# Expert stage of a fused two-layer decoder: float32 products turned into three float32r passes, and two lookup units moved

## The reference, cut to what matters

```
x = LN(x + self_attention(x))                 # layer 0, 8 heads of 8
x = LN(x + softmax(ctx x^T / sqrt(128)) .. ctx)  # layer 0, "second attention"
x = LN(x + expert(x))                         # layer 0, the stage that is changed
x = LN(x + nf4_attention_and_mlp(x))          # layer 1, weights from 4-bit codes
x = LN(x + cross_attention(x, ctx))           # layer 1
x = LN(x + ternary_mlp(x))                    # layer 1

expert(x): x W^T + b + (x A[:r]^T) B[:, :r]^T, r in (8,16,32,64) chosen per row
           by the largest of four gate scores x gate_w^T + gate_b
```

## Time and profile before

| | us |
|---|---|
| median of 3 runs | 637.84 (637.5 to 638.32) |
| profiled execution, its own time | 637.31 |
| its span | 635.5 |
| TensorE busy in the span | 623.7 |
| VectorE busy | 449.0 |
| ScalarE busy | 388.9 |
| TensorE's granted clock | 1.0 of full |

### The profile page before, as it was taken

The page is one execution under the profiler, slowest core; times in us unless marked ns, Lnnn a source line. Parts: engine busy times, 40 slices in busy tenths (PEclk is TensorE's granted clock), DMA queues, the critical chain, the costliest instruction groups (busy, mean ns, idle before and its releaser), DMA issues.

```text
span 635.5 us, 8677 instructions
## 1 busy us (share of the span) xinstructions
PE 623.7 (98%) x3186; PEld 461.7 (73%) x3186; DVE 449.0 (71%) x714; ACT 388.9 (61%) x564; POOL 64.4 (10%) x116
## 2 busy tenths in 40 slices
PE   9999999999999999999999999999999999999995
PEld 7655555544568887888888888887777888887874
DVE  4788787557778979898987537325675777777467
ACT  2977798656676697786866135223458545667532
POOL 1032132211230000000000000001221000000012
PEclk9999999999999999999999999999999999999999
DMA  7762485303133225343630003029001133200002
GB/s 251 288 214 86 168 277 199 102 0 93 48 104 108 69 77 164 122 138 99 184 108 5 1 0 135 1 92 404 1 1 33 50 101 100 67 0 2 1 34 100
DMA packets 25592, 63.94 MB, mean 101 GB/s; under 512 B 5541, under 2 KB 10725, under 8 KB 24782
## 3 DMA queue, kind: packets, MB, share of 16 engines
q1 hardware_dynamic: 23294, 61.68, 29.8%
q10 hardware_dynamic: 2256, 1.70, 0.9%
HBM read 58.77 MB, written 4.60 MB: 100 GB/s over the span
## 4 chain that ended last, share of the span: by engine, by line
PE 81%; ACT 7%; DVE 4%; DMA 4%; issue 2%; SPq 1%; POOL 0%; POOLq 0%; DVEq 0%; ACTq 0%
PE bank L1121 19%; PE bank L1257 10%; PE bank L1109 5%; PE bank L1108 5%; PE bank L1110 5%; PE bank L960 4%; PE bank L880 4%; PE bank L684 3%; ACT line L1393 3%; DMA b_gu<-in_b_gu 2%; PE bank L990 2%; PE bank L819 2%; PE bank L1199 2%; PE bank L1200 2%; PE bank L1175 1%
## 5 line engine op out<-in xcount | busy, mean ns | idle before, releaser
L1393 ACT ACTIVATE line<-line 128x1024 f32<-128x1024 f32 x87 | 91.3, 1049 | 0.1
L1108 PE MATMUL bank<-xh,wh 128*128 128x512 f32 x224 | 87.5, 391 | 0.0
L1109 PE MATMUL bank<-xl,wh 128*128 128x512 f32 x224 | 87.4, 390 | 0.0
L1110 PE MATMUL bank<-xh,wl 128*128 128x512 f32 x224 | 87.3, 390 | 0.0
L1121 PE MATMUL bank<-wh,xh 128*128 128x512 f32 x176 | 69.8, 396 | 0.2 <-DVE xl L2381 0.2
L1121 PE MATMUL bank<-wh,xl 128*128 128x512 f32 x176 | 68.6, 390 | 0.0
L2381 DVE TENSOR_TENSOR xl<-arena,xh 128x1024 fp32r<-128x1024 f32 (+1 forms) x24 | 28.3, 1178 | 35.7 <-ACT xh L1698 35.5
L1698 ACT ACTIVATE xh<-arena 128x1024 fp32r<-128x1024 f32 (+1 forms) x24 | 24.4, 1022 | 39.6 <-PE bank L1121 35.3
L1110 PEld LDWEIGHTS bank<-xh,wl 128*128 128x128 f32 x224 | 42.1, 188 | 8.9
L1108 PEld LDWEIGHTS bank<-xh,wh 128*128 128x128 f32 x224 | 42.1, 188 | 8.8 <-DVE arena L2283 0.3
L1109 PEld LDWEIGHTS bank<-xl,wh 128*128 128x128 f32 x224 | 42.1, 188 | 8.4
(11 more groups left out here) (287 smaller groups left out, 1354.3 us busy)
## 6 DMA issues: line engine op xcount, KB each, us to landing
codes<-in_c_gu SPq DMA_DIRECT2D x14, 512.0 KB, 5.2
scales<-in_s_gu SPq DMA_DIRECT2D x28, 256.0 KB, 4.0
codes<-in_t_gu SPq DMA_DIRECT2D x8, 512.0 KB, 3.8
codes<-in_c_dn SPq DMA_DIRECT2D x7, 512.0 KB, 4.9
scales<-in_s_dn SPq DMA_DIRECT2D x14, 256.0 KB, 3.9
fold<-in_t_dn SPq DMA_DIRECT2D x1, 3584.0 KB, 15.7
codes<-in_c_qkv SPq DMA_DIRECT2D x6, 512.0 KB, 4.5
scales<-in_t_gu SPq DMA_DIRECT2D x6, 512.0 KB, 4.2
```

The costliest lines, as they stand in the source:

```text
L1108: pe.matmul(dst, wh[:, s, c:c + P], xh[:, k, cols], start=(k == 0), stop=False)
L1109: pe.matmul(dst, wh[:, s, c:c + P], xl[:, k, cols], start=False, stop=False)
L1110: last = pe.matmul(dst, wl[:, s, c:c + P], xh[:, k, cols], start=False, stop=(k == KD - 1))
L1393: nc.scalar.activation(below(slot), below(slot), ACT.Prelu, bias=bias, scale=scale, alpha=alpha).then_inc(bent, 1)
```

## The change

The transposed blocks of the stage's input are written as float32r (`x2_hi`), and VectorE writes what the rounding lost (`x2_low`, into `x2_lo`). VectorE also splits the two weight matrices into high and low parts (`w0_split`, `ag_split`) during the fourth and fifth steps of the second attention. `ranks` and `ffn_W` then make three float32r passes for each of the four k (`x2_products`) in place of one float32 product. The plan of the second attention loses the units of steps 6 and 7, and the expert stage gets one more in its steps 0 and 6. `down_stack_hi` moves behind the last transposes of `attention_out`, `down_stack_low` into gate/up tile 2, and the three late down chunks each move one tile later. Buffers move too: the low parts of the attention matrix (`m_lo`) now stand where `kq_w` was, and the adapter's `ad_high` where the expert stage's input was.

```diff
-LATE = {2: 4, 5: 5, 8: 6}
+LATE = {3: 4, 6: 5, 9: 6}
...
-PLAN = ([0] + [1] * (NT - 1), [2], [0] + [1] * 7, [1] * NT)
+PLAN = ([0] + [1] * (NT - 1), [2], [0] + [1] * 5, [2, 1, 1, 1, 1, 1, 2, 1])
...
                 keys_out(t)
-                if t % 2 == 0:
+                if t in (2, 4):
                     load_scales(C_O + t // 2)
                     load_codes(C_O + 1 + t // 2)
-            load_scales(C_O + NT // 2)
...
-            for c in range(C_O + 1 + NT // 2, C_GU):
+            for c in range(C_O + NT // 2, C_GU):
+                load_scales(c - 1)
                 load_codes(c)
-                load_scales(c)
+            load_scales(C_GU - 1)
...
-                if layer == 2 and b:
-                    pe.wait_ge(xl_ready, b)
+                if NT * (layer - 1) + b > 0:
+                    pe.wait_ge(xl_ready, NT * (layer - 1) + b)
                 transpose_tile(b, x[:, b, :], bank[6])
...
+            def x2_products(dst, b, w_hi, w_lo, last):
+
+                cols = slice(b * P, (b + 1) * P)
+                part = slice(b % KD * P, (b % KD + 1) * P)
+                for k in range(KD):
+                    pe.matmul(dst, x2_hi[:, k, cols], w_hi[k], start=(k == 0), stop=False)
+                    pe.matmul(dst, x2_lo[b // KD][:, k, part], w_hi[k], start=False, stop=False)
+                    ins = pe.matmul(dst, x2_hi[:, k, cols], w_lo[:, k, :], start=False, stop=last and k == KD - 1)
+                return ins
...
-                for k in range(KD):
-                    last = pe.matmul(turn_bank(b)[:, 0:RMAX + NL], xT[:, k, b * P:(b + 1) * P], agT[:, k, :],
-                                     start=(k == 0), stop=(k == KD - 1))
-                last.then_inc(ag_ps, 1)
+                pe.wait_ge(xl_ready, max(KD, b + 1))
+                x2_products(turn_bank(b)[:, 0:RMAX + NL], b, [ag_hi[:, k, :] for k in range(KD)], ag_lo, True).then_inc(ag_ps, 1)
...
-                for k in range(KD):
-                    pe.matmul(bank[FF_BANK[b % 3]][:, :], xT[:, k, b * P:(b + 1) * P], w0T[:, k, :], start=(k == 0), stop=False)
+                x2_products(bank[FF_BANK[b % 3]][:, :], b, w0_hi, w0_lo, False)
...
-                elif t < 4:
-                    down_stack_hi(t - 2)
...
             x1_T_out(NT - 1)
+            down_stack_hi(0)
+            down_stack_hi(1)
             late_first_bends(at_gu(2))
...
+            def x2_low(b):
+
+                dve.wait_ge(xt_ready, NT + b + 1)
+                nc.vector.tensor_tensor(x2_lo[b // KD][:, :, b % KD * P:(b % KD + 1) * P], bank[6][:, :].rearrange("p (k t) -> p k t", k=KD),
+                                        f32(x2_hi[:, :, b * P:(b + 1) * P]), ALU.subtract).then_inc(xl_ready, 1)
+
+            def w0_split(rows):
+
+                for k in rows:
+                    last = nc.vector.tensor_copy(w0_hi[k], w0T[:, k, :])
+                link(last)
+                for k in rows:
+                    nc.vector.tensor_tensor(w0_lo[:, k, :], w0T[:, k, :], f32(w0_hi[k]), ALU.subtract)
+
+            def ag_split():
+
+                dve.wait_ge(in_ffn0, 48)
+                link(nc.vector.tensor_copy(ag_hi, agT))
+                nc.vector.tensor_tensor(ag_lo, agT, f32(ag_hi), ALU.subtract)
+
             for t in range(2, NT + 1):
                 if t < NT:
                     sims_max(t)
+                if t >= 3:
+                    x2_low(t - 3)
                 for u, h in half_plan(2, t, 0):
                     unit_part(u, h)
...
+                if t == 4:
+                    ag_split()
+                    w0_split(range(0, 2))
+                elif t == 5:
+                    w0_split(range(2, KD))
...
-                if t == 4:
-                    down_stack_low()
...
                 hidden(s, j - 2)
+                if j == 2:
+                    down_stack_low()
```

More of the change, by code:

```diff
@@ L217, in decoder_kernel @@
         m_hi = sb("m_hi", [P, KD, D], F32R)
+        with nc.sbuf_tensor("fold_r", [P, NF, D], F32R) as fold_r:
+            pass
         fold = sb("fold", [P, NF, D])
@@ L261, in decoder_kernel @@
         woT, at = carve(arena, at, KD * D)
+        shared_at = at
         shared, at = carve(arena, at, KD * D)
@@ L266, in decoder_kernel @@
         wo0, at = carve(arena, at, D)
+        ag_at = at
         agT, at = carve(arena, at, KD * (RMAX + NL))
@@ L271, in decoder_kernel @@
         bT_d, at = carve(arena, at, D)
+        wk2_at = at
         wk2, at = carve(arena, at, D)
@@ L287, in decoder_kernel @@
         lora_l = wo0
-        ad_high = wh[:, :, :].rearrange("p s c -> p (s c)")[:, 0:FF]
-        m_lo = [arena_r[:, m_at:m_at + D] for m_at in (wk3_at, free_at, free_at + D, wo0_at)]
+        ad_high = arena_r[:, xT_at:xT_at + FF]
+        x2_hi = arena_r[:, xT_at:xT_at + KD * T].rearrange("p (k t) -> p k t", k=KD)
+        x2_lo = [m_hi[:, :, :], wh[:, :, :].rearrange("p s c -> p (s c)").rearrange("p (k t) -> p k t", k=KD)]
+        w0_hi = [arena_r[:, w_at:w_at + D] for w_at in (wk3_at, wk2_at, free_at, free_at + D)]
+        w0_lo = arena_r[:, shared_at:shared_at + KD * D].rearrange("p (k c) -> p k c", k=KD)
+        ag_lo = arena_r[:, ag_at:ag_at + KD * (RMAX + NL)].rearrange("p (k c) -> p k c", k=KD)
         KQ_F, BETA_F, CTX_F = KD, KD + 1, NF
@@ L338, in decoder_kernel @@
         KQ_F0, CTX_SLOT = NF - 6, NF - 2
+        m_lo = [fold_r[:, KQ_F0 + c, :] for c in range(KD)]
+        ag_hi = fold_r[:, CTX_SLOT, 0:KD * (RMAX + NL)].rearrange("p (k c) -> p k c", k=KD)
         assert at <= KQ_F0 * D
@@ L496, in gu_scales_landed, with stacked @@
             eng.wait_ge(in_gus[c % RING], 32 * ((c - C_GU) // RING + 1))
+        def stacked(j, down):
+            return 2 + j + 1 + int(j >= down)
         def gu_slot(j):
@@ L636, in _ @@
                     if n >= 2:
-                        sp.wait_ge(stack_low, 3 + n - 1)
+                        sp.wait_ge(stack_low, stacked(n - 2, 3))
                     sp.dma_start(b_gu[:, n % 2, :], i["b_gu"][n]).then_inc(in_bgu[n % 2], 16)
@@ L1000, in attention_out @@
                     pe.wait_ge(x1_ready, t - 1)
-                pe.wait_ge(xl_ready, t + 1)
+                pe.wait_ge(xl_ready, NT + t + 1)
                 cols = slice(t * P, (t + 1) * P)
@@ L1050, in gu_lora @@
             def gu_lora(j):
-                pe.wait_ge(stack_low, 3 + j + 1)
+                pe.wait_ge(stack_low, stacked(j, 3))
                 if j == 0:
@@ L1070, in x1_T @@
                 elif b == 3:
-                    pe.wait_ge(xl_ready, NT)
+                    pe.wait_ge(xl_ready, 2 * NT)
                 elif b >= 4:
-                    pe.wait_ge(xl_ready, NT + b - 3)
+                    pe.wait_ge(xl_ready, 2 * NT + b - 3)
                 transpose_tile(b, rbuf[:, b % 2, :], bank[X1_BANK[b % 4]])
@@ L1098, in gu_tile @@
                     if p == 0:
-                        pe.wait_ge(xl_ready, NT + NT // 2)
+                        pe.wait_ge(xl_ready, 2 * NT + NT // 2)
                     elif p == 1:
-                        pe.wait_ge(xl_ready, 2 * NT)
+                        pe.wait_ge(xl_ready, 3 * NT)
                     else:
@@ L1211, in t_gate @@
                 if j == 0:
-                    pe.wait_ge(xl_ready, 2 * NT + (tg + 1) * NT // 2)
+                    pe.wait_ge(xl_ready, 3 * NT + (tg + 1) * NT // 2)
                 t_gu_part_of(j, tg, 0, t_ps)
@@ L1558, in _ @@
                 if t >= 2:
-                    x_T_out(NT + t - 2)
+                    x_T_out(NT + t - 2, dst=x2_hi)
                 for u, h in half_plan(2, t, 1):
@@ L2211, in add_lora @@
                 dve.wait_ge(af_ps, n + 1)
-                if n == 0:
-                    dve.wait_ge(scaled, C_DN)
+                if n in (0, KD):
+                    dve.wait_ge(scaled, C_DN - 1 + n // KD)
                 dst = (wsum, woT)[n % 2][:, n // 2, :]
@@ L2225, in down_stack_low @@
             def down_stack_low():
-                dve.wait_ge(stack_hi, 4)
+                dve.wait_ge(stack_hi, 6)
                 nc.vector.tensor_tensor(ad_st[2 * RG:STACK, :], a_down[2 * RG:STACK, :], f32(ad_high[2 * RG:STACK, :]), ALU.subtract).then_inc(stack_low, 1)
             def b_lower(j):
-                dve.wait_ge(stack_hi, 4 + j + 1)
+                dve.wait_ge(stack_hi, stacked(j, 2) + int(j >= 2))
                 part = b_st[RG:2 * RG, j % 2, :]
@@ L2250, in _ @@
             turn_norm(2 * NT - 1)
+            x2_low(NT - 2)
             choose(1)
+            x2_low(NT - 1)
             dve.wait_ge(kq_ps, NT)
```

## The result

The changed kernel is slower: 641.55 us (640.8 to 642.4) against 638.08 (637.5 to 638.64) of before on the same chip, ratio 1.005, 95% interval 1.0035 to 1.0066, some 3.5 us between the medians. Forecast were 638.9 and a range of 636.2 to 642.0. The profiled execution of after took 640.84 with a span of 639.0, 3.5 more than that of before; its granted clock is 0.999.

What follows compares the result with a forecast made beforehand. TensorE, busy 623.7 of 635.5 us, was taken as the bound. Terms -5.1 + 4.0 + 1.6 + 0.3 + 0.3 = +1.1 us gave 638.4 on the profiled execution's 637.31 and 638.9 on the median 637.84; range 636.2 to 642.0.

Steps and rivals of the forecast that it cites:

- rival D: Expert stage's first blocks: VectorE becomes the bound, steps 0 to 2 each late by a unit part; 642.2 us, chance 0.13.
- matrix and rank products: TensorE, eight blocks: twelve float32r passes replace four float32 products; matrix -5.1 us, rank +4.0 us.
- sixth context product: Second attention: the inserted splits make VectorE's probabilities late, so TensorE waits; +1.6 us, bounds nothing to 3.6.
- VectorE in steps 0 to 2: Expert stage: the moved-in chunk and shifted order delay VectorE's work against TensorE's blocks; +0.3 us, 0 to 1.
- step 6 of the expert stage: Expert stage, where the plan adds a unit: no cost forecast, 0.
- gate/up: Start of gate/up: down_stack_hi ahead of tile 2's bends delays the first hidden product; +0.3 us, 0 to 0.8.
- rival B: Rank products: short float32r passes cost 0.22 us, no cheaper than float32; +14.1 instead of +4.0, 649 us, chance 0.14.
- decides the sign from 0.12 a pass on: Rank products: pass time said to settle faster or slower from 0.12 us, each 0.01 making 0.96 us.
- From step 3 on ... VectorE waits for TensorE again.: Expert stage: each block holds 3.4 us more attention_product and down_stack_low (2.02) is gone, so VectorE has room.
- `down_stack_low` ... follows behind the hidden product in a tile that no longer has the late chunk's 3.7: Gate/up: the 2.02 us subtraction goes where the 3.7 us late chunk left; no cost of its own forecast.
- The later LATE positions only swap neighbours: Gate/up: moving the later late down chunks was taken as mere reordering, with no cost or gain forecast.
- wait at a second place for more than a microsecond: TensorE, anywhere besides the sixth context product: such a wait was named as a sign that the forecast is wrong.

Runs made afterwards that it cites:

- e9: Changed kernel with down stack back in the expert stage, step 6's second unit in step 3, splits in second-attention steps 5 and 6: ratio 0.9943 to before.
- e4: Changed kernel with the weight splits in steps 5 and 6 of the second attention instead of 4 and 5: ratio 1.0029 to before.
- e3: Changed kernel with the second unit of the expert stage's step 6 moved to step 3: ratio 1.0032 to before.
- e2: Changed kernel with the down stack's copies and subtraction back in the expert stage, steps 2 to 4: ratio 1.0006 to before.
- e6: Kernel before with only the changed LATE positions, {3: 4, 6: 5, 9: 6}: ratio 0.9981 to before.
- e1: Changed kernel with LATE back as before, {2: 4, 5: 5, 8: 6}: ratio 1.0134 to before.

## Why the prediction was right or wrong

The direction and the number came out inside what was stated, 641.55 in 636.2 to 642.0, but in good part by luck. The upper end of the range was the sum of rival D, which didn't happen; two losses that the sum had at 0 and at +0.3 took its place, and products that came cheaper than forecast offset some of them.

The forecast's +1.1 against the +3.48 of the marks, term by term:

| term | forecast | measured | from |
|---|---|---|---|
| matrix and rank products | -5.1 + 4.0 = -1.1 | -1.8 | e9 against before: 0.42 in A, 1.34 in B |
| sixth context product | +1.6 | +1.57 | A, after against e4 |
| VectorE in steps 0 to 2 | +0.3 | 0 | B saves 0.22 a block without a wait, as A does |
| step 6 of the expert stage | 0 | +1.1 | B, after against e3 |
| gate/up | +0.3 | +2.54 | D, after against before: +3.3 for the stack (e2), -0.8 for `LATE` (e6) |

**Passes.** Right in kind, a little small in size. A rank pass takes 0.111 us against the 0.115 taken; the rank blocks came at 1.28 behind a matrix block, under the 1.32 to 1.44 named, and at 1.36 behind transposes, and rival B of the forecast (0.22 a pass) is out. A matrix block is 2.85 us, forecast 2.80, but what it replaced was 3.54 where adapter products stand ahead of it, and I had taken 3.44 from a block behind rank products. The net saving of a block is 0.22 us and not 0.14. The forecast's remark that B "decides the sign from 0.12 a pass on" doesn't follow from its own terms: with the waits it forecast, the sum is nil at 0.104 a pass, and without them at 0.126.

The Trainium skill (TensorE: Matmul & The Clock Gate, LDWEIGHTS) gives an estimate of 0.107 us a load; the trace, with 0.111, agrees. By the Trainium skill (FP8 and Floating Point Precision, TensorE Precision Notes) a matrix block would be 2.58 us, an estimate; the trace has 2.85 and decides.

**The second attention.** Right to a tenth: `sims_max(5)` at 105.96 (forecast 105.9), probabilities ready at 110.08 (110.15), the wait 1.34 in the row and 1.57 in the stage. It wasn't repeated at steps 6 and 7, and nothing later gave it back.

**"From step 3 on ... VectorE waits for TensorE again."** This failed. The plan has a second unit in step 6 as in step 0. Its joins run when the last `attention_product` is done, and step 7 has none. I costed the unit in step 0 and not that in 6. The runs put 1.1 us there (e3).

**"`down_stack_low` ... follows behind the hidden product in a tile that no longer has the late chunk's 3.7"** and **"The later LATE positions only swap neighbours"**. This is the step that cost most, 2.2 us of the 2.4 by which the sum was off. I followed the late bends to the first bank they hold up and forecast +0.3 there; the row says 0.16 of idle time, and the products stand 0.54 apart where 0.23 is usual. I stopped at that bank. VectorE's work came 3.5 us late at the join of tile 2 and 3.9 late at the additions into fold: first in its own queue, with the subtraction, up to the split of tile 2 (0.60), then through the late transfer and ScalarE's bends to the additions (1.80). Both are waits of TensorE. With the first they make the 3.3 us that e2 takes out of D, by distances between starts. That no chunk was left in tile 2 was right, and worth 3.9 us in D (e1 against after), but the chunk went to tile 3, where the delay met it. Nor do the late chunks only swap neighbours: in before the swap gains 1.2 us (e6), since the additions behind the chunk of tile 6 are done in time, 0.6 us before they are needed, where those of tile 5 were late.

Rival D named the kind (VectorE bound in the first expert blocks, 642.2) and came near the number for another reason: those blocks had no wait at all in after. That TensorE would wait at a second place for more than a microsecond was named as what would make the forecast wrong, and it did, at 253: by its own sign the forecast's mechanism was incomplete, though its number held.

## What to carry to other kernels

When side work is moved, follow the delay until it is gone, through every consumer in the queue of the engine that takes it and through the transfers that it lets start, and not only to the first bank that comes late; each unit in a plan's table has to be set against its own step's cover. Passes that win a microsecond on the bound engine can lose three by where their side work stands: the arithmetic was 1.8 us to the good here, and three moves of the same instructions turned +0.5% into -0.6%. Where a large and a small transfer are issued together and the small one is waited for first, try issuing it first: it gained 1.1 and 1.5 us in two kernels here, and nothing in e9, where no wait was left.

## What the runs showed of the hardware

A float32r pass of 112 columns starts every 0.111 us and a float32 product of the same shape every 0.22, in two records 0.11 apart; passes of 256 and 512 columns start every 0.120 and 0.233. The page counts one weight load for each record, 3250 of both in after. That the load sets the time at 112 columns is read from this, as transposes of 128 columns start every 0.110 too. Float32 blocks of 512 columns took 3.44 us behind rank products and 3.54 behind adapter products. A 96 KB transfer issued behind 512 KB of codes was used 4.9 us after its issue in one execution and 6.6 in another, with the same issue time; at the same point of the program, ScalarE's wait for it was 5.55 and 7.98 us, and 2.77 and 3.62 with the transfer issued first. A GpSimd instruction on one column took 0.57 us, and 1.59 where it started together with a VectorE join of 1,024 columns (186.86 beside 186.80 in after; all seven kernels with the double unit in step 6 show it, and the other seven don't). The rows show that the two go together; why wasn't tested.
